# A graph network on one core: a wait for the last group's landing ahead of each four indirect DMAs

## The reference

```python
x = _layernorm(x + _L0_gnn_ref(x, src, dst, ...))         # three SAGE layers
x = _layernorm(x + _L1_gnn_ref(x, edge_index, ...))       # two attention layers, a mean over neighbours
x = _layernorm(x + _L2_gnn_ref(x, src, dst, ...))         # four convolutions, the maximum over them
x = _layernorm(x + _L3_gnn_ref(x, edge_index, ...))       # three convolutions
# each layer holds a sum over edges of this kind:
agg = jax.ops.segment_sum(h[src], dst, num_segments=N)
```

## Time and profile before

| | |
|---|---|
| median of 3 runs | 8025.8 us (8025.77 to 8031.93) |
| span of the profiled execution | 7959.6 us, 87265 instructions |
| PE / PEld busy | 4974.4 (62%) / 3347.6 (42%) |
| DVE busy | 4628.0 (58%) |
| ACT busy | 3052.7 (38%) |
| POOL (GpSimd) busy | 3976.5 (50%), 3991 instructions |
| DMA | 1292.17 MB, mean 162 GB/s; GpSimd's queue 14.7% and SyncE's 39.9% of 16 engines |
| place scatter L821 | x196, mean 988 ns |
| place gather L1135 | x196, mean 946 ns |
| gathers L573 | x588 of jk_layer1 to 3, mean 1010 ns; x196 in each other block, 947 to 1040 ns |

### The profile page before, as it was taken

How to read it: one execution, slowest core, us unless ns; L and a number is a source line. 1 busy time by engine, 2 the same in 40 slices (tenths; PEclk the granted TensorE clock), 3 DMA queues, 4 the chain that set the end, 5 groups by cost and what they waited for, 6 DMA issues and landing times. The chain is left out here.

```text
span 7959.6 us, 87265 instructions
## 1 busy us (share of the span) xinstructions
PE 4974.4 (62%) x23924; PEld 3347.6 (42%) x23924; DVE 4628.0 (58%) x13648; ACT 3052.7 (38%) x6979; POOL 3976.5 (50%) x3991
## 2 busy tenths in 40 slices
PE   6888189529798992457633344343499996569211
PEld 4565057316455870157522222221255554346111
DVE  5666068403334662576767445565699996555444
ACT  3444056316332320144434333342477774236000
POOL 5666700450443437465565556566433333655666
PEclk9999599769898885569755567676699998789555
DMA  5776145329675652169644346674577775556332
GB/s 190 249 247 231 16 158 202 106 62 295 208 244 182 202 153 53 43 174 257 196 118 123 102 122 121 109 133 87 128 248 251 251 251 185 173 180 195 85 88 75
DMA packets 1104142, 1292.17 MB, mean 162 GB/s; under 512 B 133903, under 2 KB 815679, under 8 KB 1097390
## 3 DMA queue, kind: packets, MB, share of 16 engines
q1 hardware_dynamic: 973518, 1032.63, 39.9%
q0 software_dynamic: 130144, 253.97, 14.7%
HBM read 607.93 MB, written 682.10 MB: 162 GB/s over the span
## 5 line engine op out<-in xcount | busy, mean ns | idle before, releaser
L573 POOL DMA_INDIRECT jk_layer_msg<-jk,idx_jk x588 | 593.7, 1010 | 371.4 <-issue 173.1
L1057 PE MATMUL jk_layer_sum_ps<-ident,jk_layer_weighted 128*128 128x128 f32 x784 | 175.1, 363 | 736.1 <-ACT jk_layer_weighted L1023 386.5
L1057 PEld LDWEIGHTS jk_layer_sum_ps<-ident,jk_layer_weighted 128*128 128x128 f32 x784 | 112.1, 180 | 845.7 <-ACT jk_layer_weighted L1023 435.3
L2084 POOL TENSOR_TENSOR rows_moved<-rows_x_in,w_lonely_row 128x512 f32<-128x512 f32 x98 | 124.7, 1273 | 674.3 <-DVE rows_x L674 638.8
L1079 DVE TENSOR_TENSOR_SCAN jk_layer_sum_t<-goes_on,jk_layer_sum_t,jk_layer_sum_ps 128x512 f32<-128x512 uint8 x196 | 250.1, 1276 | 350.7 <-DMA sage_nodes_x_in<-in_x 285.2
L573 POOL DMA_INDIRECT sage_msg<-h,idx x196 | 185.7, 947 | 485.4 <-POOLq L137 272.5
L1196 DVE COPY sage_h<-sage_turn 128x512 f32<-128x512 f32 x98 | 67.8, 691 | 608.5 <-PE sage_turn L690 400.5
L1886 ACT ACTIVATE jk_layer_h_t<-jk_layer_h_ps,w_jk_b 128x512 f32<-128x512 f32 x196 | 134.7, 687 | 622.5 <-DMA gat_own<-yv 322.2
L699 PE MATMUL sage_nodes_h_ps<-sage_nodes_h_t,w_ws 128*128 128x512 f32 x784 | 363.6, 607 | 0.0
L699 PE MATMUL sage_h_ps<-sage_sum_t,w_wn 128*128 128x512 f32 x588 | 295.6, 612 | 95.3 <-issue 93.5
L894 ACT ACTIVATE sage_nodes_h_t<-sage_nodes_h_ps,w_b_c 128x512 f32<-128x512 f32 x392 | 248.8, 688 | 253.1 <-PE sage_nodes_h_ps L699 140.1
(11 more groups left out here) (457 smaller groups left out, 16621.0 us busy)
## 6 DMA issues: line engine op xcount, KB each, us to landing
h<-sage_nodes_h SPq DMA_DIRECT2D x196, 512.0 KB
h_t<-sage_h_t SPq DMA_DIRECT2D x98, 512.0 KB
h<-sage_h SPq DMA_DIRECT2D x98, 512.0 KB
jk_t<-jk_layer_h_t SPq DMA_DIRECT2D x196, 256.0 KB
rows_layers<-jk_t SPq DMA_DIRECT2D x49, 1024.0 KB, 5.9
r<-rows_h SPq DMA_DIRECT2D x98, 512.0 KB
second_x_in<-u SPq DMA_DIRECT2D x147, 260.0 KB
jk<-jk_layer_h SPq DMA_DIRECT2D x147, 256.0 KB
```

The costliest lines, as they stand in the source:

```text
L573: pool.indirect_dma_start(out=into[:, g.number % depth, s, :], out_offset=None, in_=table, in_offset=bass.IndirectOffsetOnAxis(ap=index_ti ...
L1057: mm = pe.transpose(ps[:, c, at_s], self.weighted[:, g.b, s, c * P:(c + 1) * P], self.K.ident[:])
L2084: pool.tensor_tensor(moved[:, g.b], x_in[:, g.number % 3], to_subs(W.lonely_row), ALU.add).then_inc(lonely_added.sem, 1)
```

## The change

Every group of four indirect DMAs named above, but for the counts and the scatter to the output, now has a wait for the group before it in the same stream (`g.lag(1)`): all 16 increments of each of its four DMAs. Where 196 DMAs went out in one loop they now go by groups of four with four semaphores in rotation. The order of instructions on each engine is the same as before, and so are all data and buffers; the other four engines' programs are unchanged. Semaphores aside, GpSimd's row of operations reads word for word the same.

```diff
+UNLANDED = 1
 def pool_gather(pool, g, index_tile, used, table, into, arrived):
     depth = len(arrived.sems)
     wait_for(pool, used, g.lag(depth))
+    wait_for(pool, arrived, g.lag(UNLANDED))
     for s in range(SUB):
         pool.indirect_dma_start(out=into[:, g.number % depth, s, :], ...).then_inc(arrived.of(g), 16)
...
 # fetch_block
-        for t in range(ET):
-            pool.indirect_dma_start(out=kept[:, t, :], ...).then_inc(arrived[t % 4], 16)
-        for sem in arrived:
-            pool.wait_ge(sem, 16 * (ET // 4))
+        for r in range(EG):
+            g = Group(r)
+            wait_for(pool, arrived, g.lag(UNLANDED))
+            for t in range(SUB * r, SUB * (r + 1)):
+                pool.indirect_dma_start(out=kept[:, t, :], ...).then_inc(arrived.of(g), 16)
+        wait_for_all(pool, arrived)
...
 # sage_nodes_block, after pool.wait_ge(places_set, 16); the same form in slot_hidden_block with places_in
-        for t in range(ET):
-            pool.indirect_dma_start(out=tables["place"], ...).then_inc(places_done, 16)
-        pool.wait_ge(places_done, 16 * ET)
+        for r in range(EG):
+            g = Group(r)
+            wait_for(pool, placed, g.lag(UNLANDED))
+            for t in range(SUB * r, SUB * (r + 1)):
+                pool.indirect_dma_start(out=tables["place"], ...).then_inc(placed.of(g), 16)
+        wait_for_all(pool, placed)
...
 # second_product_block
             if r >= 4:
                 wait_for(pool, turned, Group(4 * (r - 4)))
+            wait_for(pool, fetched, g.lag(UNLANDED))
```

More of the change, by code:

```diff
@@ L577, in fetch_block @@
 def fetch_block(nc, name, K, table, kept, counts_table):
-    ph = Phase(nc, name, 0)
-    arrived = [ph.sem(f"arrived{b}") for b in range(4)]
+    ph = Phase(nc, name, EG)
+    arrived = ph.dma_sems("arrived", SUB, 4)
     counts = SourceCounts(ph, K, counts_table)
@@ L600, in _ @@
     def _(pool):
-        for t in range(ET):
-            pool.indirect_dma_start(out=kept[:, t, :], out_offset=None, in_=table,
-                                    in_offset=bass.IndirectOffsetOnAxis(ap=K.idx[:, t:t + 1], axis=0)).then_inc(arrived[t % 4], 16)
-        for sem in arrived:
-            pool.wait_ge(sem, 16 * (ET // 4))
+        for r in range(EG):
+            g = Group(r)
+            wait_for(pool, arrived, g.lag(UNLANDED))
+            for t in range(SUB * r, SUB * (r + 1)):
+                pool.indirect_dma_start(out=kept[:, t, :], out_offset=None, in_=table,
+                                        in_offset=bass.IndirectOffsetOnAxis(ap=K.idx[:, t:t + 1], axis=0)).then_inc(arrived.of(g), 16)
+        wait_for_all(pool, arrived)
     ph.close()
@@ L750, in sage_nodes_block @@
     node_no = ph.sb("node_no", [P, NODES_PAD // P], I32)
-    nodes_ready, places_set, places_done = ph.sem("nodes_ready"), ph.sem("places_set"), ph.sem("places_done")
+    nodes_ready, places_set = ph.sem("nodes_ready"), ph.sem("places_set")
+    placed = DmaSems([ph.sem(f"placed{b}") for b in range(4)], SUB, EG)
     fetch_done, stashed = ([DmaSems([ph.sem(f"{k}{n}_{b}") for b in range(2)], per, EG) for n in range(2)] for k, per in (("fetch_done", SUB), ("stashed", 1)))
@@ L818, in _ @@
         pool.wait_ge(places_set, 16)
-        for t in range(ET):
-            pool.indirect_dma_start(out=tables["place"], out_offset=bass.IndirectOffsetOnAxis(ap=K.idx_out[:, t:t + 1], axis=0),
-                                    in_=K.slot_no[:, t:t + 1], in_offset=None, bounds_check=N_NODES - 1, oob_is_err=False).then_inc(places_done, 16)
-        pool.wait_ge(places_done, 16 * ET)
+        for r in range(EG):
+            g = Group(r)
+            wait_for(pool, placed, g.lag(UNLANDED))
+            for t in range(SUB * r, SUB * (r + 1)):
+                pool.indirect_dma_start(out=tables["place"], out_offset=bass.IndirectOffsetOnAxis(ap=K.idx_out[:, t:t + 1], axis=0),
+                                        in_=K.slot_no[:, t:t + 1], in_offset=None, bounds_check=N_NODES - 1, oob_is_err=False).then_inc(placed.of(g), 16)
+        wait_for_all(pool, placed)
         for n in range(2):
@@ L1096, in slot_hidden_block @@
         own, own_arrived, own_turned = ph.sb("own_rows", [P, 2, SUB, D]), A_("own_arrived"), S("own_turned")
-        places_in = ph.sem("places_in")
+        places_in = A_("places_in", SUB, 4)
         own_ps = ph.ps("own_ps", [P, GROUP])
@@ L1133, in _ @@
         if first:
[L1134 to L1137, removed]
+            for r in range(EG):
+                g = Group(r)
+                wait_for(pool, places_in, g.lag(UNLANDED))
+                for t in range(SUB * r, SUB * (r + 1)):
+                    pool.indirect_dma_start(out=K.place[:, t:t + 1], out_offset=None, in_=tables["place"],
+                                            in_offset=bass.IndirectOffsetOnAxis(ap=K.src_node[:, t:t + 1], axis=0)).then_inc(places_in.of(g), 16)
+            wait_for_all(pool, places_in)
         else:
```

## The result

The changed kernel takes 8294.6 us (median of 4 runs, 8288.1 to 8311.1) for 8025.8: 1.034 of the time, with a 95% interval of 1.032 to 1.035. It is slower; the forecast was 7944 us, and the time lies above its range. The profiled execution has a span of 8309.3 us.

What follows compares the result with a forecast made beforehand. GpSimd's pace was taken to bound many blocks, its unbroken runs two stretches, TensorE and DMA the rest. Costs of 258 less 180 and 160 gave -82: 7878 us on the span, 7944 with 66.2 added; range 7740 to 8180.

Steps and rivals of the forecast that it cites:

- The starved stretches: Beside the scatter in sage_nodes and the gather of places in sage0, pauses free the other engines: -180 and -160 us.
- W: GpSimd's pause from the end of a group's fourth issue to the next group's first start, sized by block.
- the scatter's longer end is covered: In sage_nodes, the scatter growing from 257 to 353 us delays nothing, as GpSimd has nothing due until the last node groups.
- W lies between 1.6 and 3.1: Pause bounds in us, taken from other engines' waits for landings and sage_nodes; set by block from its DMA share.
- What is late is word from one engine to another: Beside unbroken indirect DMAs, signals between engines, not work, come late, by about a tenth of the run's length afterwards.
- The tails: Way from the last landing to the next block: 15 us in jk_layer0 and gcn0, 22 in mean, 33 in gcn1.
- fetch: GpSimd takes 314 + 3 us for 314, and the counts come well inside it: 0, with -3 to +5 us.
- sage1, sage_end: Both already pause, sage1 4.0 us and longer than W, sage_end with little to spare: +10 us for both.
- The 66 us: The runs' median lies 66.2 us above the profiled span, so 7878 us on the span becomes 7944 us.
- Rival 1: Pauses free nobody, so the two stretches only get longer, by 96 and 100 us: +454, 8480 us; chance 0.12.
- Rival 2: W is 3.1 us everywhere, 7.9 us a group: +286, 8312 us; no change from about W = 2.6; chance 0.18.
- only sage_nodes shows such a value: Argument against W of 3.1 us everywhere: the other blocks move half the bytes of sage_nodes.

Runs made afterwards that it cites:

- before_again: The kernel before, unchanged, profiled once more: a span of 8053.0 us in an execution of 8054.9 us.
- two_stretches: The changed kernel with the new waits kept only in the scatter of slot numbers and the gather of places: 7750.7 us, 0.966 of before.
- jk_store_late: The changed kernel, but in jk_layer0 to 2 SyncE stores h_t only once h is ready too: 8238.5 us, 1.027 of before.
- lag_two: The changed kernel with UNLANDED = 2, so GpSimd waits for the group before the last one: 7954.1 us, 0.993 of before.

## Why the prediction was wrong

- **The starved stretches** (right in kind, -340 us forecast, -259 measured by the timelines). The neighbours came back to life as said: TensorE at 86% beside the scatter and at 98% until 1223 us, a slot group at 5.4 us. sage_nodes ended 136 us earlier, where 180 were forecast: the node groups beside the scatter were quicker than forecast (10.6 us for 13.2), but the scatter took 541 us instead of 353 (W 6.0 for 2.3), and "the scatter's longer end is covered, since GpSimd has nothing due until the last node groups" failed: those last groups were due at 1223 us and stood until 1288. Four groups at 10.6 us from 1223 on would have ended the block at about 1265 (an estimate), where it ended at 1352. Besides, 49 groups were left at the scatter's start instead of 43. That comes from the quick execution and not from the change: 50 were done in the first 698 us of before_again, 49 in 708 of two_stretches, which has no wait there. sage0 lost 123 instead of 160: 374 us of gathers for 348 (W 3.0 for 2.3), with a tail of 22 for 12.
- **The step that failed** is "W lies between 1.6 and 3.1", and in it the rows that it rests on. 1.6 and 2.25 us are the first groups of their blocks, with no store and one wait, and they are the readers' starts: GpSimd's own pauses in the same two states are 1.85 and 2.43. The share of DMA was used to go between them, and it doesn't order the blocks: second with the highest share (0.87) has 3.9, but jk_layer0 with 0.46 has 3.6 and gcn0 with 0.55 has 2.3. What the runs showed in its place: a GpSimd that starts from each landing meets the same store each time, 1.4 us in jk_layer0 (jk_store_late); the shared row is 0.8 us in jk_layer1 to 3, and the store of h another 0.3 in two of them; the second wait is 0.5 us from the fourth or fifth pause on. For second (3.9), gcn1 (3.4) and the start of the scatter no run shows what makes the pause long. In gcn1 the first gather of each group also takes 1.33 us for 0.95 beside VectorE's join. By block the lengths miss by +88 (jk_layer0), +113 (jk_layer1 to 3), +56 (gcn1), +49 (second), +33 (mean), +19 (fetch), +12 (gcn_end), +5 (gcn0), +44 (sage_nodes), +37 (sage0), and -30 (sage1 and sage_end, forecast at +10 and measured at -20). With +5 us in the blocks between, the sum is 431, which is 8309 for 7878.
- **"What is late is word from one engine to another"** holds for the hand-over in fetch, though its row names no releaser ([2.20 <-issue]). VectorE's instruction for that matmul ended at 3100.56 us and the matmul started at 3102.00, 1.4 us later:

```profile
3100.32 0.24 DVE L532 TENSOR_SCALAR fetch_hi_hot<-hi_iota,src_hi 128x128 bf16<-128x128 bf16 x1
```

  Why an unbroken row of indirect DMAs makes it late, no run shows.
- **The tails** were sized well: 17 us behind the last gather in jk_layer0 (15), 24 in mean (22), 18 in gcn0 (15).
- **fetch** was to cost nothing. The counts were freed (161 of 196 matmuls in the first 100 us, 76 before), but GpSimd set the end and every pause counted: +19.
- **sage1, sage_end**: right that the pauses hide, wrong in sign; the blocks won 20 us.
- **The 66 us** between span and median were rightly added, since the medians of the kernel before stay at 8025 to 8042 us. The fault is that the blocks' lengths were read from a quick execution. Of the 431 us some 64 are that, and 17 more that the profiled execution of the changed kernel was the slowest of its four (8311.1 us); the miss on medians is 351 us. In second the same code took 410 to 438 us in six profiles, so a good part of its +49 is spread.
- **The rivals.** Rival 1 is out: lag_two has waits without pauses and starves, the changed kernel has pauses and doesn't. Rival 2 gave 8312 us for a median of 8295, and its point of no change, W = 2.6, has most blocks above it. But it was priced at one W for all, where the measured ones go from 1.9 to 6.0, and its sum leaves out fetch, which at 7.9 us a group would add some 76 us. Its time is right largely by luck. It had 0.18; the argument against it ("only sage_nodes shows such a value") took a row that is missing for a row that speaks against.

The Trainium skill, DMA: Bandwidth & Descriptors, section "Queues, rings and completion order", says that a DMA's last descriptor, which raises the semaphore, lands only after every earlier write of that DMA engine, across its queues. That would make a gather's landing wait for a store already on the same engines, and the direction of jk_store_late agrees with it in jk_layer0 (3.6 us with a store half a us ahead of the gather's end, 2.2 with the same store 3.6 us ahead of it). But the packets of the trace show the gather's data itself late (2.8 us behind the gather's end for 1.2), with the 4-byte packets ending within 0.01 us of it in both kernels, so the order of the increment isn't shown to be the cause; no run shows the order inside one DMA engine.

## What to carry to other kernels

A pause is worth what the neighbours gain in it and costs its length only where GpSimd sets the end of the block, so decide block by block, and choose its frequency so that GpSimd and its neighbours end together (here eight DMAs beside the slot groups, four in sage1, none in the jk layers). When a wait ties an engine to its own transfers, don't size it from landings that were measured while the engine ran free: look for the transfer that the last landing sets off, and for where it will stand when the next one lands. Ask what the slowed engine still owes to others behind its stream: here two small memsets behind the scatter held the last four node groups for 65 us. And take a second profile of the kernel before, so that the quick blocks of one execution aren't taken for the usual ones.

## What was not expected of the hardware

- A scatter of 4 bytes per row makes GpSimd wait 4.0 us for its landing (67.6 us in 17) with nothing beside it and 1.9 at its end, where a gather of 512-byte rows has 1.85 from the first; beside other traffic it waits up to 14.9 us. What makes the wait shrink along the scatter is open.
- Four gathers of which many rows are one and the same land 0.6 us later at a block's start (2.43 for 1.83 us of pause) and 0.8 later on (jk_layer3).
- Two waits ahead of a gather make it start 0.5 us later after the landing than one does, though the second was met long before (1.07 us from the last packet for 0.6).
- A gather that starts together with VectorE's 0.69 us instruction on the same landing takes 1.28 us instead of 0.94; beside ScalarE's it doesn't (0.95).
